# Second attention: the negative maxima as three more rows of the contraction instead of selection matmuls

## What is computed

```python
def _L0_attn_b_ref(x, wq, w_down, wk_up, wv_up, wo):
    q = (x @ wq).reshape(B, T, H, D)
    lat = x @ w_down
    k = (lat @ wk_up).reshape(B, T, H, D)
    v = (lat @ wv_up).reshape(B, T, H, D)
    q, k = _apply_rope(q, cos, sin), _apply_rope(k, cos, sin)
    scores = jnp.einsum('bqhd,bkhd->bhqk', q, k) * scale
    allowed = pages[None, :] <= pages[:, None]
    scores = jnp.where(allowed[None, None], scores, jnp.finfo(scores.dtype).min)
    attn = jax.nn.softmax(scores, axis=-1)
    out = jnp.einsum('bhqk,bkhd->bqhd', attn, v).reshape(B, T, E)
    return out @ wo
x = x + _L0_attn_a_ref(_layernorm(x), ...)
x = x + _L0_ffn_ref(_layernorm(x), ...)
x = x + _L0_attn_b_ref(_layernorm(x), ...)
x = x + _L0_ffn_ref(_layernorm(x), ...)
```

## Time and profile before

| what | us |
|---|---|
| median of 3 runs | 572.63 (571.8 to 573.14) |
| the profiled execution | 575.24 |
| its span in the trace | 573.4 |
| TensorE busy | 423.3 (74% of the span) |
| VectorE busy | 324.9 (57%) |
| ScalarE busy | 211.7 (37%) |
| GpSimd busy | 202.3 (35%) |
| granted TensorE clock, mean | 0.857 |

### The profile page before, as it was taken

The page is one execution under the profiler, slowest core; times in us unless marked ns, Lnnn a source line. Parts: engine busy times, 40 slices in busy tenths (PEclk is TensorE's granted clock), DMA queues, the critical chain, the costliest instruction groups (busy, mean ns, idle before and its releaser), DMA issues.

```text
span 573.4 us, 14608 instructions
## 1 busy us (share of the span) xinstructions
PE 423.3 (74%) x4870; PEld 315.7 (55%) x4871; DVE 324.9 (57%) x1042; ACT 211.7 (37%) x483; POOL 202.3 (35%) x299
## 2 busy tenths in 40 slices
PE   2768878788872599955467899999888763999900
PEld 2646666666662377743135666766666652677800
DVE  2555656775666445426865576668776664444412
ACT  1445645544530022211135657655665400222200
POOL 3132335443445100027666335633612442000054
PEclk9968989998775699995567999999999955899965
DMA  8999200000000111111100000000000001111123
GB/s 271 348 337 296 83 2 13 11 5 5 10 11 27 29 55 53 50 38 37 27 0 2 1 2 3 0 0 0 1 2 10 29 19 32 39 53 54 41 70 90
DMA packets 40896, 30.91 MB, mean 54 GB/s; under 512 B 3344, under 2 KB 37008, under 8 KB 40592
## 3 DMA queue, kind: packets, MB, share of 16 engines
q1 hardware_dynamic: 32176, 23.06, 13.2%
q0 software_dynamic: 2048, 4.20, 2.5%
q10 hardware_dynamic: 6624, 3.02, 1.8%
HBM read 15.26 MB, written 15.01 MB: 53 GB/s over the span
## 4 chain that ended last, share of the span: by engine, by line
PE 56%; DVE 15%; issue 8%; POOL 7%; ACT 7%; DMA 4%; SPq 1%; ACTq 0%; DVEq 0%; POOLq 0%
PE S L1311 8%; PE bank L1324 7%; PE bank L1194 6%; POOL yg L1042 4%; PE S L1317 4%; PE S L1235 3%; PE S L1401 3%; ACT E L910 3%; PE bank L1354 3%; PE S L1402 2%; PE bank L1211 2%; DVE nmax L491 2%; PE bank L1414 2%; PE bank L1377 2%; PE bank L1154 2%
## 5 line engine op out<-in xcount | busy, mean ns | idle before, releaser
L829 ACT ACTIVATE E<-S,nmax 128x256 f32<-128x256 f32 x128 | 59.1, 478 | 59.7 <-DVE nmax L491 59.7
L1042 POOL DMA_INDIRECT yg<-slots,pos x32 | 30.8, 963 | 141.3 <-DMA slots<-yo 132.8
L872 ACT ACTIVATE hT<-S 128x512 f32<-128x512 f32 x46 | 27.5, 597 | 106.6 <-PE S L1317 106.6
L1003 POOL TENSOR_TENSOR vs<-Va,rden 128x512 f32<-128x512 f32 x32 | 33.3, 1040 | 80.1 <-DVE rden L520 77.2
L910 ACT ACTIVATE E<-S 128x1536 f32<-128x1536 f32 x32 | 46.4, 1450 | 25.7 <-PE S L1405 25.7
L1311 PE MATMUL S<-W,xgT 128*128 x92 | 52.3, 652 | 0.0
L677 DVE TENSOR_REDUCE nm<-bank 128x2 f32<-128x512 f32 x64 | 41.1, 684 | 16.1 <-PE bank L1377 16.1
L491 DVE TENSOR_REDUCE nmax<-S 128x4 f32<-128x1024 f32 x32 | 39.1, 1221 | 17.6 <-PE S L1235 16.6
L1324 PE MATMUL bank<-W,hT 128*128 x368 | 48.5, 276 | 0.0
L1324 PEld LDWEIGHTS bank<-W,hT 128*128 128x128 f32 x368 | 44.7, 192 | 0.1
L1148 PE MATMUL bank<-cst,xnb 128*128 128x128 f32 x44 | 11.9, 369 | 40.5 <-DVE xnb L415 29.6
(11 more groups left out here) (169 smaller groups left out, 1010.8 us busy)
## 6 DMA issues: line engine op xcount, KB each, us to landing
slots<-zeros SPq DMA_DIRECT2D x1, 8640.0 KB, 38.0
xg<-slots SPq DMA_DIRECT2D x46, 64.0 KB, 1.8
slots<-yo ACTq DMA_DIRECT2D x46, 64.0 KB, 1.6
W<-in_L_ffn_W SPq DMA_DIRECT2D x1, 2048.0 KB, 10.5
b<-in_L_ffn_b SPq DMA_DIRECT2D x1, 2048.0 KB, 20.1
x<-in_L_attn_a_x SPq DMA_DIRECT2D x4, 256.0 KB, 3.6
yg<-in_select SPq DMA_DIRECT2D x1, 1024.0 KB, 8.1
out<-x SPq DMA_DIRECT2D x8, 128.0 KB, 2.2
```

The source lines that it names most:

```text
L829: last = act.activation(E[:, hp, h, c, :], S[hp % 2][:, h, c * T:(c + 1) * T], ACT.Exp, bias=nmax[:, hp, k:k + 1], accum_out=den[:, hp, k: ...
L1042: pool.indirect_dma_start(out=yg[:, t, :], out_offset=None, in_=xs_dram, in_offset=bass.IndirectOffsetOnAxis(pos[:, t:t + 1], 0)).then_inc ...
```

## The change

- `b_scoresT` loses the selection matmuls. The three bf16 parts of a head's negative maxima are written into rows 56 to 58 of its 64 in `qT`, which were zero; the same rows of the keys' mask are now 1, so that the one matmul of keys and queries adds them. `b_scores` reads the same tiles earlier, while the rows are still zero.
- The rows get there by DMA on SP's queue, `b_maxima_rows`, between the tile loads of the two feed-forwards: per sequence and half (two quarters, i = 0 and 1) six DMAs of 4 x 256 bf16, from four partitions of `mT` to one of `qT`. Semaphores `mrow0` and `mrow1`; `b_scoresT` waits for them at quarters 0 and 2.
- The maxima are therefore handled in two halves: `b_maxima(b, i)` on GpSimd, 16 columns of `nm` each, into `ms[:, i]`; `b_mt(b, i)` on TensorE, two transposes each; and the copy to `mT`, half 0 on VectorE, half 1 on ScalarE. Half 0 of b+1 is in the middle of round b, behind `b_scoresT(b, 2)` and ahead of `b_scores(b+1, 2)`, which waits for the copy since both use `pb[2]`. Half 1 is where the whole was.
- `in_select` holds the masks (128 x 64) instead of the selection matrix, `cst` loses them (727 columns instead of 791), and `copies` has five steps instead of nine.

```diff
+            def b_maxima_rows():
+                for b in range(B):
+                    for i in range(2):
+                        sp.wait_ge(bs["mT"], b * 2 + i + 1)
+                        for h in range(2):
+                            for k in range(3):
+                                r = 64 * h + 56 + k
+                                j = (h * 3 + k) * 4
+                                sp.dma_start(qT[r:r + 1, b % 2, 4 * i:4 * i + 4, :], mT[j:j + 4, i, :]
+                                             ).then_inc(bs[f"mrow{i}"], 16)
             ffn_loads(0)
+            b_maxima_rows()
             ffn_loads(1)
...
             def b_max(b, q):
-                if q == 0:
-                    waits(dve, bs["ms"], b)
+                if q % 2 == 0:
+                    waits(dve, bs["ms"], 2 * b - 1 + q // 2)
...
-                if n: b_max(b + 1, 2)
+                if n:
+                    dve.wait_ge(bs["mt"], b * 2 + 3)
+                    waits(dve, bs["mrow0"], (b + 1) * 96)
+                    dve.tensor_copy(mT[:, 0, :], pb[2][0:24, 0:P].bitcast(BF16)).then_inc(bs["mT"], 1)
+                    b_max(b + 1, 2)
...
                 if n:
-                    act.wait_ge(bs["mt"], b + 2)
-                    act.copy(mT[:, :, :], pb[2][:, 0:P].bitcast(BF16).rearrange("p (u t) -> p u t", u=2)
-                             ).then_inc(bs["mT"], 1)
+                    act.wait_ge(bs["mt"], b * 2 + 4)
+                    waits(act, bs["mrow1"], (b + 1) * 96)
+                    act.copy(mT[:, 1, :], pb[2][0:24, 0:P].bitcast(BF16)).then_inc(bs["mT"], 1)
...
+                if there(b + 1):
+                    b_maxima(b + 1, 0)
                 if there(b + 4):
                     pool.wait_ge(bs["latT"], b + 3)
                     b_stage(b + 4, p)
                 if there(b + 1):
-                    b_maxima(b + 1)
+                    b_maxima(b + 1, 1)
...
             def b_scores(b, p, q):
+                if q % 2 == 0:
+                    waits(pe, bs["mT"], b * 2 + q // 2)
...
             def b_scoresT(b, p, q):
-                if q == 0:
-                    pe.wait_ge(bs["mT"], b + 1)
+                if q % 2 == 0:
+                    pe.wait_ge(bs[f"mrow{q // 2}"], (b + 1) * 96)
                 waits(pe, bs["exp"], b * 4 + q)
                 for d in range(2):
                     for h in range(2):
-                        n, hh = 2 * q + d, 4 * q + 2 * d + h
-                        dst = S4[:, d, h * T:(h + 1) * T]
-                        pe.matmul(dst, kT[:, p, n, h, 0:P], qT[:, p, n, :], start=True, stop=False)
-                        pe.matmul(dst, sel[:, hh, :], mT[:, :, :], start=False, stop=True)
-                        dst = S4[:, 2, (2 * d + h) * P:(2 * d + h + 1) * P]
-                        pe.matmul(dst, kT[:, p, n, h, P:T], qT[:, p, n, P:T], start=True, stop=False)
-                        last = pe.matmul(dst, sel[:, hh, :], mT[:, 1, :], start=False, stop=True)
+                        n = 2 * q + d
+                        pe.matmul(S4[:, d, h * T:(h + 1) * T], kT[:, p, n, h, 0:P], qT[:, p, n, :], start=True, stop=True)
+                        last = pe.matmul(S4[:, 2, (2 * d + h) * P:(2 * d + h + 1) * P], kT[:, p, n, h, P:T],
+                                         qT[:, p, n, P:T], start=True, stop=True)
                 last.then_inc(bs["st"], 1)
+            def b_mt(b, i):
+                pe.wait_ge(bs["ms"], b * 2 + i + 1)
+                for u in range(2):
+                    last = pe.transpose(pb[2][0:24, 0:P].bitcast(BF16)[:, u * P:(u + 1) * P], ms[:, i, u, :], identb[:, :])
+                last.then_inc(bs["mt"], 1)
...
-                if n: b_scores(b + 1, 1 - p, 2)
+                if n:
+                    b_mt(b + 1, 0)
+                    b_scores(b + 1, 1 - p, 2)
```

More of the change, by code:

```diff
@@ L1577, in _select @@
 def _select():
[L1579 to L1582 removed]
+    page = np.arange(T)[:, None] // PAGE
+    pages = np.arange(NPG)[None, :]
+    zero = np.zeros((T, 8))
+    qmask = np.concatenate([np.where(page < pages, MASKED, 0.0), zero], 1)
+    kmask = np.concatenate([page == pages, zero], 1)
+    kmask[:, NPG:NPG + 3] = 1.0
+    return np.concatenate([m for c in (qmask, kmask) for m in (c[:P], c[P:])], 1).astype(np.float32)
 CST, NCST = {}, 0
```

62 lines of the change are left out of this document (25 added, 37 removed).

## The result

The changed kernel took 585.01 us (median of 5 runs, 583.77 to 591.51), the kernel before 572.63 us beside it (5 runs): a ratio of 1.023 [1.019, 1.028]. The prediction was 570.2 us and its range ended at 573.8. Run again beside other kernels it took the same: 585.02 us (4 runs), ratio 1.023 [1.018, 1.028]. Medians here are over all runs of a kernel; the ratios leave out two long runs at a lower clock, one of e9 (594.83 us) and one of e10 (567.53), without which their medians are 583.28 and 562.18.

What follows compares the result with a forecast made beforehand. TensorE comes first but not alone; in the changed rounds GpSimd's split and the relay behind it hold it. +0.8 - 1.4 - 0.1 + 0.8 - 0.5 - 1.9 - 0.1 = -2.4 us: 570.2 us, range 566.0 to 573.8.

Steps and rivals of the forecast that it cites:

- the relay: Mid-round: maxima split on GpSimd, transposed on TensorE, copied on VectorE before b_scores(b+1, 2); 2.17 us, its start 0.63 later.
- marks in the prediction's list: b_split to ms 0.3 us; TensorE idle over 1; rounds 1-4 near 19.06; round 7 near 17.2; rounds -1, 5 longer.
- wrong if: Rounds 0-7: clock under 1.00 in new places, TensorE waiting for mrow, or rounds 1-4 shrinking by a microsecond.
- third rival: TensorE's clock falls in the new idle time: up to 1.7 us a fall, four give some 577; chance 12%.
- the sum: All rounds of the last attention plus the smaller constants: -2.4 us in total, giving 570.2 us.
- decides from two falls on: From two falls of TensorE's clock on, at up to 1.7 us each, the third rival would decide the result.
- four operations: GpSimd's small operations on half the maxima, within the relay: taken at 1.0 us, between 0.57 and 1.13 or somewhat more.
- second rival: The relay costs 0.4 to 0.5 us more than 2.17; six rounds lose 2.5 us, about 572.5; chance 20%.
- Round 7: No relay there; router ranks, ScalarE's copy and router logits behind b_scoresT each move by 0.6 us: -1.9 us.
- That decides: GpSimd's new maxima step stands behind b_split, so it can't start sooner; rounds 1 to 4 change by -0.1 us in all.
- first rival: GpSimd isn't the bound in the middle, VectorE's maxima are; rounds 1 to 4 give 1.2 us each, 565.6; chance 10%.
- ceiling: Matmuls removed from b_scoresT on TensorE: 2.64 us a round, 21 us in all, if nothing stood beside it.

Runs made afterwards that it cites:

- e9: e1 with TensorE waiting ahead of b_scores(b+1, 2) for the first half's maxima and the xb copy, no work added; 583.67 us, ratio 1.022.
- e10: e1 plus six useless 512-column matmuls in round -1, ahead of the second half's transposes; 562.94 us, ratio 0.984.
- e2: The changed kernel plus six useless 512-column matmuls ahead of the first half's transposes in each round; 584.07 us, ratio 1.016.
- e7: The changed kernel with the b_scoresT matmuls of quarters 0 and 1 issued twice; 580.81 us, ratio 1.017.
- e6: The kernel before the change with the selection matmuls of b_scoresT left out and nothing in their place; 565.33 us, ratio 0.990.
- e12: e1 run again unchanged; 564.38 us, ratio 0.988.
- after: The changed kernel itself, against the kernel before; 585.01 us, ratio 1.023.
- e1: The changed kernel with the first half's transposes moved to bank 1 behind b_values(b, 1), so b_scores(b+1, 2) doesn't wait for them; 566.07 us, ratio 0.987.
- e4: The changed kernel with every b_scoresT matmul issued twice; 586.29 us, ratio 1.022.

## Why the prediction was wrong, point by point

**Places and mechanism.** The first small operation on `ms` comes 0.32 behind the split's last, TensorE idles over 1 us ahead of the transposes, the relay turns the savings of the first three quarters into a wait, and the rows land in time. Of the marks in the prediction's list the first two and the last came true (the 0.3 us, the idle time, rounds -1 and 5 longer). Rounds 1 to 4 within 0.3 of 19.06 did not: 19.39 and more. Rounds 7 and 8 grew together, and the clock fell in them. Of its "wrong if" the first came true, the clock under 1.00 in new places.

**The step that failed is the third rival's chance: the sum puts a fall of the clock behind the new wait at nothing.** The rival had the mechanism, the place and nearly the price: 1.37 to 1.59 us a fall in rounds 2 to 4, "up to 1.7" forecast. It got 12% since 58 to 62 us, busy 1.78 us of 4, had kept its clock, and one stretch which kept it was taken as weighing against falls in eight rounds. By the table above a round with over 2 us of this idle time had a fall in 11 of 17 cases, and each of the three profiles that have it in all of rounds 1 to 5 had two to four falls in them. So "decides from two falls on" was the likely case and not one in eight. The falls cost 4.5 us in rounds 2 to 4 (three of them, over the 19.39 of round 1) and 2.2 in round 5 (22.25 against e2's 20.05 at full clock): 6.7 of the 14.4 us by which the sum missed. The Trainium skill, TensorE: Matmul & The Clock Gate, "HAM oscillation", cited there for this rival, tells of a kernel whose waits for DMA of some 3 to 5 us bring the clock down again and again. The trace agrees in kind, but with shorter waits: 1.48 + 0.66 us a round, and the clock fell.

**The relay was 0.34 us too cheap.** Term by term in round 2: wait 0.32 (0.30), four operations 1.15 (1.0), to TensorE 0.10 (0.10), transposes 0.28 (0.28), to VectorE 0.13 (0.06), copy 0.28 (0.29), back 0.25 (0.14). The sum, 2.51 for 2.17, is the whole lengthening of a round at full clock: +0.33 measured, -0.03 forecast. That is the second rival's mechanism at somewhat less than its price, and it costs 1.4 us in rounds 1 to 4 and about 0.8 in round 5 (+1.6 at full clock, +0.8 forecast). Both 1.4 and 0.8 are estimates, from round 1 and from e2's round 5. The four operations on half the elements cost as much as four on all of them, 1.13; that bound had been named and the value between was taken.

**Round 7 had the wrong sign.** Forecast -1.9; rounds 7 and 8 together +2.5. Two of the three savings of 0.66 do arrive at first. TensorE's wait for the router's `pos`, before, in the changed kernel and in e7 (round 7 starts at 438.97, 445.61 and 445.03):

```profile
450.70 0.61 PE L1154 MATMUL bank<-wg,xnTb 128*128 128x8 f32 x4 [0.40 <-DVE pos L451]
...
452.44 0.37 ACT L914 COPY vs<-bank 128x256 f32<-128x256 f32 x1 [0.38 <-PE bank L1417]
```

```profile
456.02 1.02 PE L1176 MATMUL bank<-wg,xnTb 128*128 128x8 f32 x4 [1.06 <-DVE pos L464]
...
459.06 0.37 ACT L931 COPY vs<-bank 128x256 f32<-128x256 f32 x1 [1.10 <-PE bank L1444]
```

```profile
456.75 0.61 PE L1176 MATMUL bank<-wg,xnTb 128*128 128x8 f32 x4 [1.05 <-DVE pos L464]
```

The matmuls behind this wait start 10.41 us into the round, where they started 11.73 us in: 1.32 sooner. The third 0.66 has turned into wait, 1.06 for 0.40; in e7, which has only quarters 2 and 3 halved, it does the same at full clock (11.72 us in, wait 1.05). So the router's work on VectorE takes one of the three, which the prediction counted in full. The clock takes the rest: it falls 10.2 us into round 7, where before it fell at 460.3, 21.3 us in, and ScalarE's `vs` starts 13.45 us in, before 13.47. e6, which has no relay and no row DMAs, falls at nearly the same place, 10.5 us in, after the same 84 matmul records (the two pieces of round 7 above), and e12 10.1 us in, with 42.4 us for the two rounds. e7, with its doubled matmuls, keeps 1.00 for 23 us in round 7, and the two rounds take 38.4. So here it isn't the relay: with half of `b_scoresT` gone TensorE stands in thinner work among the router's steps and loses its clock earlier. That agrees in these kernels, but the point of the fall also moves: 6 us into round 7 in the first profile of after and 7 in e1, 2 in e2, and e4, with all of `b_scoresT` doubled, has a fall 14 us in. What sets it is argued, not shown. The prediction never asked whether the clock would last.

**"That decides" held, but only for this place of the relay.** A round that GpSimd doesn't hold, the first rival's case, was priced at -1.2; with the relay out of the middle it is -1.85 (e1) and with no relay -2.13 (e6). The prediction took the relay's place as given, and called its 2.64 us a round a ceiling of which little would arrive; that without this one wait four fifths of it arrive is what it missed.

**Small terms.** To the end of round -1 +1.1 (forecast +0.8; +3.4 in the first profile), round 0 -0.9 (-1.4), round 6 -0.2 (-0.5). DMA issues 0.57 for 0.44 us: wrong and without effect. Two slips of arithmetic change nothing: for round 0 the prediction's own terms, -0.9 and -0.66, give -1.6 and not -1.4, and the second rival's -2.4 + 2.5 is +0.1 and not -0.1. The sum of the six pieces is +12.1, of the forecast for them -2.3.
